# Weights of the last expert layer loaded into free places, two sets during the first expert layer, and their splits moved

## What is computed

```python
def _L2_ffn_ref(x, gate_w, w1, w2, w3, sw1, sw2, sw3):      # first expert layer
    scores = jax.nn.softmax(xf @ gate_w.T, axis=-1)
    topw, topi = jax.lax.top_k(scores, TOP_K)
    h = jax.nn.silu(jnp.einsum('td,eid->tei', xf, w1)) * jnp.einsum('td,eid->tei', xf, w3)
    h = h * comb[:, :, None]
    y = jnp.einsum('tei,edi->td', h, w2)
    z = jax.nn.silu(xf @ sw1.T) * (xf @ sw3.T) @ sw2.T
...
def _L3_attn_ref(x, w_qkv, b_qkv, w_out, b_out):            # attention layer
    attn = jax.nn.softmax(jnp.einsum('bqd,bkd->bqk', q, k) * scale, axis=-1)
    out = jnp.einsum('bqk,bkd->bqd', attn, v)
    return out @ w_out + b_out
...
def _L3_ffn_ref(x, Wr, Wi, bi, Wo, bo):                     # last expert layer
    topk_vals, topk_idx = jax.lax.top_k(router_logits, TOP_K)
    h = jnp.einsum('th,efh->etf', xf, Wi) + bi[:, None, :]
    h = jax.nn.gelu(h, approximate=False)
    expert_out = jnp.einsum('etf,ehf->eth', h, Wo) + bo[:, None, :]
```

## Time and profile before

| | |
|---|---|
| median of 3 runs | 1121.81 us |
| profiled execution, its own time | 1123.41 us |
| its span | 1121.6 us |
| mean granted clock of TensorE | 0.814 of 2.4 GHz |
| PE busy | 869.2 us (77%) |
| DVE busy | 811.3 us (72%) |
| ACT busy | 600.2 us (54%) |
| POOL busy | 341.9 us (30%) |
| DMA moved | 117.88 MB, mean 105 GB/s |
| the attention layer lies at | 896.5 to 976.6 us |
| the last layer begins at | 976.9 us |

### The profile page before, as it was taken

The page is one execution under the profiler, slowest core; times in us unless marked ns, Lnnn a source line. Parts: engine busy times, 40 slices in busy tenths (PEclk is TensorE's granted clock), DMA queues, the critical chain, the costliest instruction groups (busy, mean ns, idle before and its releaser), DMA issues. The chain is left out here.

```text
span 1121.6 us, 17427 instructions
## 1 busy us (share of the span) xinstructions
PE 869.2 (77%) x6016; PEld 586.7 (52%) x6016; DVE 811.3 (72%) x1730; ACT 600.2 (54%) x1009; POOL 341.9 (30%) x337
## 2 busy tenths in 40 slices
PE   7689999986999665577663287999999386557992
PEld 3333333342589512233361265998888344457991
DVE  6589999984754489999937864888886445473763
ACT  2755454412477377799934144677773054265660
POOL 0026666633066122222100023222222600034335
PEclk9889999997999655555556578999999776769995
DMA  8086665503000000000000181999990274302653
GB/s 268 23 229 157 174 173 155 141 1 85 1 1 3 19 0 1 0 1 1 1 1 1 43 238 62 255 267 258 267 265 24 57 194 132 101 26 65 227 203 88
DMA packets 61735, 117.88 MB, mean 105 GB/s; under 512 B 10256, under 2 KB 37456, under 8 KB 61648
## 3 DMA queue, kind: packets, MB, share of 16 engines
q1 hardware_dynamic: 58576, 110.48, 35.1%
q0 software_dynamic: 3072, 6.30, 1.8%
HBM read 91.09 MB, written 16.81 MB: 96 GB/s over the span
## 5 line engine op out<-in xcount | busy, mean ns | idle before, releaser
L459 POOL TENSOR_TENSOR hC<-hs,Cb 128x1024 f32<-128x1024 f32 x47 | 110.9, 2359 | 124.0 <-DVE hs L498 124.0
L498 DVE TENSOR_TENSOR_SCAN hs<-ps_l,dBu 128x1024 f32<-128x1024 f32 x48 | 110.0, 2291 | 2.8 <-ACT ps_l L590 1.2
L658 PE MATMUL ps_l<-hC,selT 128*96 128x512 f32 x192 | 93.3, 609 | 1.5 <-POOL hC L459 1.5
L590 ACT ACTIVATE ps_l<-d_sp,Am 128x1020 f32<-128x1020 f32 x48 | 53.5, 1115 | 71.5 <-DVE hs L498 71.3
L643 PE MATMUL ps_l<-du,sel 96*128 96x512 f32 x192 | 90.5, 593 | 1.4 <-DVE dBu L491 1.4
L1900 POOL CAST m_h_hi<-m_h 128x512 f16<-128x512 f32 x54 | 49.1, 910 | 139.3 <-DVE m_h L1975 139.3
L2304 PE MATMUL ps_m<-m_wd_hi,m_h_hi 128*128 128x192 f16 x248 | 62.3, 251 | 7.3 <-issue 4.0
L1986 DVE TENSOR_TENSOR m_h_lo<-m_h,m_h_hi 128x512 f16<-128x512 f32 x62 | 42.8, 691 | 34.0 <-POOL m_h_hi L1900 31.0
L2191 ACT ACTIVATE m_act<-ps_m 128x512 f32<-128x512 f32 x62 | 36.8, 593 | 56.8 <-PE ps_m L2286 50.9
L1585 PE MATMUL ps_l<-q_xi,identh 128*128 128x512 f16 x48 | 28.5, 595 | 48.9 <-DVE q_ex L1340 28.1
L1213 POOL TENSOR_SCALAR q_e<-q_qi 128x512 int16<-128x512 f16 x48 | 30.0, 625 | 119.1 <-ACT q_qi L1480 60.6
(11 more groups left out here) (543 smaller groups left out, 2862.5 us busy)
## 6 DMA issues: line engine op xcount, KB each, us to landing
d_sp<-scan_d SPq DMA_DIRECT2D x48, 512.0 KB, 4.5
m_sta<-in_m_ua SPq DMA_DIRECT2D x25, 512.0 KB, 4.3
m_stb<-in_m_ub SPq DMA_DIRECT2D x50, 256.0 KB, 5.7
m_std<-in_m_dn SPq DMA_DIRECT2D x25, 384.0 KB, 6.0
gw_dn_in<-gw_dn SPq DMA_DIRECT2D x10, 576.0 KB, 3.3
gw_dn_in<-in_g_dn SPq DMA_DIRECT2D x8, 576.0 KB, 5.5
scratch_x<-zero SPq DMA_DIRECT2D x1, 4416.0 KB, 19.6
m_xg<-scratch_x SPq DMA_DIRECT2D x23, 192.0 KB, 5.9
```

Source lines behind the costliest of these rows:

```text
L459: pool.tensor_tensor(hC[:, n % 2, :], hs[:, n % 2, :], Cb[:, which(n), :], ALU.mult).then_inc(weighted, 1)
L498: v.tensor_tensor_scan(hs[:, n % 2, ::step], dA(n)[:, ::step], dBu[:, n % 2, ::step], 0.0, ALU.mult, ALU.add).then_inc(scanned, 1)
L590: act.activation(dst[:, :, o:o + L - 1], d_sp[:, n % NSP, :].rearrange("p (b t) -> p b t", t=L)[:, :, o:o + L - 1], ACT.Exp, scale=Am[:, c ...
L658: mm = pe.matmul(ps[0:DI, 6 + half, :], selT[:, n % NG, :], hC[:, n % 2, half * BANK:(half + 1) * BANK], start=(n == STEPS), stop=(m == ST ...
```

## The change

The two staging places are allocated before the first expert layer, and sets 0 and 1 are loaded into them by SP during that layer, right after its last own weight set. Sets 2, 3 and 4 are loaded at the start of the attention layer, as raw float32 into the final places of experts 7, 6 and 5 (`raw`, `places`); sets 5, 6 and 7 use the staging places again. Splitting set 5, 6 or 7 overwrites the raw data of set 4, 3 or 2, so its high parts wait for the low parts of those. All 24 splits are now made in the attention layer: high 0 to 2 before the norm's square root, 3 to 5 after the row turns, 6 to 13 one after each evacuation, 14 to 17 before the image loop, 18 to 23 one in each n; low 0 to 13 before the a_v adds, 14 and 15 after them, 16 to 19 one for each image behind its copy, 20 and 21 at n = 5, 22 and 23 at n = 6 behind the last residual add. In the last layer the splits go, `G_DIRECT` becomes 6, and each direct block has a one-hot place of its own, made three blocks ahead.

```diff
-def expert_layer(nc, K, X, D, ln, pre, use, routed, tiles, gated, out=None):
+def expert_layer(nc, K, X, D, ln, pre, use, routed, tiles, gated, R, out=None):
...
                     while ahead < sets and begins[ahead - NST] <= b - 1:
                         load(ahead)
                         ahead += 1
+                        if ahead == sets:
+                            for n in range(2):
+                                R.load(sync, D, n)
...
-G_DIRECT = 5
+G_DIRECT = 6
-G_LATE = 18
...
+    def places(self, ctx):
         self.up = ctx.sb("gw_up", [P, GE, 4, GU], F16)
         self.dn = ctx.sb("gw_dn", [P, GE, 2, GD], F16)
         self.bias = ctx.sb("gw_bias", [P, GE, GT])
+
+    def raw(self, w):
+        if w in (2, 3, 4):
+            up = self.up[:, 9 - w, :, :].rearrange("p a c -> p (a c)").bitcast(F32)
+            dn = self.dn[:, 9 - w, :, :].rearrange("p a c -> p (a c)").bitcast(F32)
+        else:
+            up = self.up_in[w in (1, 6)][:, :, :].rearrange("p a c -> p (a c)")
+            dn = self.dn_in[w in (1, 6)][:, :]
+        return up[:, 0:GU], up[:, GU:2 * GU], dn
 
     def load(self, sync, D, w):
-        a = w % 2
-        if w >= 2:
-            sync.wait_ge(self.lo_done, 3 * (w - 1))
+        if w >= 5:
+            sync.wait_ge(self.lo_done, {5: 3, 6: 6, 7: 18}[w])
...
     def high(self, act, n):
+        w, i = divmod(n, 3)
         src, hi, lo = self.parts(n)
-        act.wait_ge(self.w_in[n // 3 % 2], 64 * (n // 6 + 1))
+        act.wait_ge(self.w_in[w], 64)
+        if w >= 5:
+            act.wait_ge(self.lo_done, 3 * (9 - w) + 3)
         act.activation(hi, src, ACT.Copy, scale=WS).then_inc(self.hi_done, 1)
...
                 def one_hot(b):
-                    if b >= 2:
-                        v.wait_ge(turned, b - 1)
...
-                    if G_LATE + b < 3 * GE:
-                        R.low(v, G_LATE + b)
                     low(2 * b)
-                    if 2 <= b + 2 < G_DIRECT:
-                        one_hot(b + 2)
+                    if b + 3 < G_DIRECT:
+                        one_hot(b + 3)
...
-                for n in range(G_LATE, 3 * GE):
-                    R.high(act, n)
...
             def _(sync):                                   # attention layer
-                for w in range(2):
+                for w in range(2, 5):
                     R.load(sync, D, w)
                 sync.dma_start(R.bias[:, :, :], D["g_b"].rearrange("(e p) f -> p e f", p=P)).then_inc(R.bias_in, 16)
                 clear_last(sync, K)
-                for w in range(2, GE):
+                for w in range(5, GE):
                     R.load(sync, D, w)
...
-                for n in range(8):
+                for n in range(14):
                     R.low(v, n)
                 for q in range(NT // 2):
                     v.wait_ge(vals, q + 1)
                     v.tensor_tensor(vt[:, 2 * q:2 * q + 2, :], ...
-                    if q in (1, 3):
-                        R.low(v, 8 + q // 2)
+                for n in range(14, 16):
+                    R.low(v, n)
...
                         v.tensor_copy(PT[:, b % 2, :, :], ...
+                        R.low(v, 15 + n)
...
-                    for i in range(10 + 2 * n, min(12 + 2 * n, G_LATE)):
-                        R.low(v, i)
+                    if n >= 5:
+                        for i in range(2 * n + 10, 2 * n + 12):
+                            R.low(v, i)
...
             def _(act):
+                for n in range(3):
+                    R.high(act, n)
                 ln.scalar(act, use)
                 tr.scalar(act, use - 2, uT, ps)
+                for n in range(3, 6):
+                    R.high(act, n)
...
-                        if n >= 1:
-                            R.high(act, n - 1)
-                for n in range(7, 10):
+                        R.high(act, 6 + n)
+                for n in range(14, 18):
                     R.high(act, n)
```

More of the change, by code:

```diff
@@ L2360 @@
 G_BLOCKS = GE + G_OVER
-G_DIRECT = 5
+G_DIRECT = 6
 G_TRIO = 3 * P
-G_LATE = 18
 class LastWeights:
     def __init__(self, ctx):
+        self.up_in = [ctx.sb(f"gw_up_in{a}", [P, 2, GU]) for a in range(2)]
+        self.dn_in = [ctx.sb(f"gw_dn_in{a}", [P, GD]) for a in range(2)]
+        self.w_in = [ctx.sem(f"gw_in{w}") for w in range(GE)]
+        self.bias_in = ctx.sem("gw_bias_in")
+        self.hi_done, self.lo_done = ctx.sem("gw_hi"), ctx.sem("gw_lo")
+    def places(self, ctx):
         self.up = ctx.sb("gw_up", [P, GE, 4, GU], F16)
@@ L2379, in load @@
     def load(self, sync, D, w):
-        a = w % 2
-        if w >= 2:
-            sync.wait_ge(self.lo_done, 3 * (w - 1))
-        sync.dma_start(self.up_in[a][:, 0, :], D["g_ua"][w * CA:(w + 1) * CA, :]).then_inc(self.w_in[a], 16)
+        if w >= 5:
+            sync.wait_ge(self.lo_done, {5: 3, 6: 6, 7: 18}[w])
+        a, b, d = self.raw(w)
+        sync.dma_start(a, D["g_ua"][w * CA:(w + 1) * CA, :]).then_inc(self.w_in[w], 16)
         for half in range(2):
-            sync.dma_start(self.up_in[a][half * CB:(half + 1) * CB, 1, :], D["g_ub"][w * CB:(w + 1) * CB, :]).then_inc(self.w_in[a], 16)
@@ L2386, in load @@
-        sync.dma_start(self.dn_in[a][:, :], D["g_dn"][w * P:(w + 1) * P, :]).then_inc(self.w_in[a], 16)
+            sync.dma_start(b[half * CB:(half + 1) * CB, :], D["g_ub"][w * CB:(w + 1) * CB, :]).then_inc(self.w_in[w], 16)
+        sync.dma_start(d, D["g_dn"][w * P:(w + 1) * P, :]).then_inc(self.w_in[w], 16)
     def parts(self, n):
         w, i = divmod(n, 3)
-        if i < 2:
-            return self.up_in[w % 2][:, i, :], self.up[:, w, 2 * i, :], self.up[:, w, 2 * i + 1, :]
-        return self.dn_in[w % 2][:, :], self.dn[:, w, 0, :], self.dn[:, w, 1, :]
+        hi, lo = (self.dn[:, w, k, :] if i == 2 else self.up[:, w, 2 * i + k, :] for k in range(2))
@@ L2394, in high @@
+        return self.raw(w)[i], hi, lo
     def high(self, act, n):
+        w, i = divmod(n, 3)
         src, hi, lo = self.parts(n)
-        act.wait_ge(self.w_in[n // 3 % 2], 64 * (n // 6 + 1))
+        act.wait_ge(self.w_in[w], 64)
+        if w >= 5:
+            act.wait_ge(self.lo_done, 3 * (9 - w) + 3)
         act.activation(hi, src, ACT.Copy, scale=WS).then_inc(self.hi_done, 1)
@@ L2424, in last_layer @@
         seat = ctx.sb("g_seat", [P, NT, GE])
-        hot = ctx.sb("g_hot", [P, 2, NT, P], F16)
+        hot = ctx.sb("g_hot", [P, G_DIRECT, NT, P], F16)
         lg = ctx.sb("g_lg", [P, NT, GE])
@@ L2576, in one_hot @@
                 def one_hot(b):
-                    if b >= 2:
-                        v.wait_ge(turned, b - 1)
                     for t in range(NT):
-                        v.tensor_scalar(hot[:, b % 2, t, :], slots1[:, :], seat[:, t, b:b + 1], None, ALU.is_equal).then_inc(hot_ready, 1)
+                        v.tensor_scalar(hot[:, b, t, :], slots1[:, :], seat[:, t, b:b + 1], None, ALU.is_equal).then_inc(hot_ready, 1)
                 def copy_up(d):
@@ L2643, in _ @@
                 one_hot(1)
+                one_hot(2)
                 v.wait_ge(placed, 2)
@@ L2770, in turn @@
                                 mm = pe.matmul(ps[:, 4 + b % 2, part * P:(part + 1) * P], U16[:, t, part * P:(part + 1) * P],
-                                               hot[:, b % 2, t, :], start=(t == 0), stop=(t == NT - 1))
+                                               hot[:, b, t, :], start=(t == 0), stop=(t == NT - 1))
                     else:
@@ L2965, in _ @@
                                            accum_out=sums[:, 2 * b + q:2 * b + q + 1]).then_inc(expd, 1)
+                        R.high(act, 18 + n)
+                    else:
+                        R.high(act, 18 + n)
                     if n >= 2:
@@ L2972, in _ @@
                                        ACT.Copy).then_inc(out_sb, 1)
-                    for i in range(10 + 2 * n, min(12 + 2 * n, G_LATE)):
-                        R.high(act, i)
             @block.tensor
@@ L3064, in program @@
             quantised_layer(nc, K, X, D, ln)
+        R = LastWeights(ctx)
         if LAYERS > 3:
-            expert_layer(nc, K, X, D, ln, "m", 1, 16, 4, True)
-        R = LastWeights(ctx)
+            expert_layer(nc, K, X, D, ln, "m", 1, 16, 4, True, R)
+        R.places(ctx)
         if LAYERS > 4:
```

## The result

The changed kernel takes 1132.26 us (median, 1130.72 to 1133.03) against 1121.76 (1121.34 to 1123.26) of the kernel before: ratio 1.0092, 95% interval 1.0069 to 1.0115: slower, by just under one per cent. The forecast was 1129.1. Its profiled execution has a span of 1130.8 us, 9.2 more than the 1121.6 of before. One execution among all runs of this document, one of ten of after_dve_dummies (experiment 5), took 3362.59 us, and its ratio leaves that one out.

| us | before | after | difference | predicted |
|---|---|---|---|---|
| first expert layer ends | 896.46 | 908.22 | +11.8 | +11.1 |
| attention layer | 80.44 | 69.52 | -10.9 | -5.0 |
| last layer | 144.7 | 153.06 | +8.4 | +1.2 |
| sum | | | +9.2 | +7.3 |

The account below looks back on a forecast made before the run. It took PE as the bound once DMA ran empty in the first expert layer, a PE, DVE, ACT ring in attention, PE late in the last layer. +11.1 - 5.0 + 1.2 = +7.3 on 1121.81 gave 1129.1 us, range 1117 to 1133.

Parts of the forecast that it names:

- Part 1: First expert layer: two sets loaded ahead of the last m_xg make PE stand 8.9 us, then restart slowly; +11.1 us.
- the restart at the lower clock: First expert layer, behind PE's stall: PE restarts at half clock, costing 1.9 to 3.3 us, taken as 2.2.
- early loads hide: Rival, first expert layer: m_xg is served beside the 2.75 MB, so PE never waits; 1118.0 us, chance 0.14.
- Part 2: Attention layer: loading sets 2, 3, 4 and moving splits gives -9.0 in the rounds, +3.5 at the tail; taken as -5.0.
- the DVE splits (4.2): Attention layer, third and fourth rounds: splits no longer hold DVE ahead of what PE waited for; -4.2 us.
- The tail: Attention layer's end: DVE's splits 20 to 23 around the last add put +3.5 us in front of the block's end.
- The warning signs named: Signs of a wrong forecast, among them set 7 or set 4 arriving late and holding ACT before exp or OT.
- Part 3: Last layer: removed splits count 0, block 5 built by 24 matmuls instead of 3 transposes costs +1.2 us.
- the six low splits of DVE in the loop lie in PE's shadow: 0: Last layer's loop: removing DVE's six low splits changes the time by 0, at most -1 us.
- nothing gained: Last layer: the wait on all scatters moves one block later, but block 5 was turned after it; 0.
- a rival of +4: Last layer: block 5's direct turn lengthens a stretch with unexplained idle time, +4 instead of +1.2; 1132 us, chance 0.08.
- the likeliest case: Whole kernel: the forecast itself, 1129.1 us, own range 1125 to 1132.5, chance 0.72.

Follow-up runs that it names:

- after_dve_dummies: Changed kernel plus six useless DVE instructions of a low split's size in the last layer's blocks 0 to 5: 1128.33 us, ratio 1.0054.
- experiment 5: Third-chip runs: loads_behind_rows, after_direct5 and all_gaps repeated, plus after_dve_dummies; ratios 0.9967, 1.0069, 0.9968 and 1.0054.
- experiment 1: Two, one or no early weight sets put ahead of the first expert layer's last rows: ratios 1.0106 (kernel before otherwise), 0.9877 and 0.9819 (changed kernel otherwise).
- before_again: The kernel before, unchanged, profiled again on the second chip: 1122.11 us (one execution).
- before_early_loads: Kernel before with only weight sets 0 and 1 loaded early, in the first expert layer instead of the attention layer: 1131.73 us, ratio 1.0106.
- second set: Runs on the second chip, among them before_again, after_again and all_gaps, beside the kernel before at a median of 1122.96 us.
- first set: Runs on the first chip, among them before_early_loads, loads_behind_rows and after_direct5, beside the kernel before at a median of 1120.42 us.
- after_direct5: Changed kernel with G_DIRECT back at 5 instead of 6: 1118.31 us, ratio 0.998; repeated on the third chip 1129.8 us, ratio 1.0069.
- loads_behind_rows: Changed kernel with both early weight sets issued behind the last routed block's rows and that step's store: 1100.61 us, ratio 0.9819.
- third set: Runs on the third chip, those of experiment 5, beside the kernel before at a median of 1122.59 us.
- all_gaps: Changed kernel with early sets behind the last rows, first high splits behind the square root, tail low splits in DVE's idle time: 1113.68 us, ratio 0.9922.
- after_again: The changed kernel, unchanged, run again on the second chip: 1132.73 us, ratio 1.0085 against the kernel before.
- loads_behind_second: The kernel of loads_behind_rows repeated on the third chip: 1117.6 us, ratio 0.9967 against the kernel before.

## Why the prediction was right, and where it was not

**Part 1, right.** Each step of it shows in rows. m_xg went out at 838.57 (named: near 839), landed at 852.5 (computed 851.4), PE idled 9.68 (8.9), the layer ended 11.8 later (11.1). What is left of 11.8 behind the stall is 2.1, which I put down to the restart at the lower clock (2.2). The rival "early loads hide" needed a landing before 845. The rule of the Trainium skill ("DMA: Bandwidth & Descriptors", section "Queues, rings and completion order") that each DMA engine consumes descriptors in ring order agrees with the dose of experiment 1: 8.8 to 9.7, 4.0 and no stall for two, one and no sets ahead. The advice in the same page of the Trainium skill, section "Rules for kernel authors", to issue early and wait late, holds here only for loads that have nothing urgent behind them on their queue. Where the loads went behind the rows, it held: ratio 0.982 and 0.997 in two sets.

**Part 2, right in its steps up to the first round, too small behind it.** Counted from the layer's start, to which 11.76 are added: the projections came 0.96 later (+0.9), the scores stood at 928.16 (927.9), exp at 933.31 (933.1), the first transposes 5.25 earlier (4.8). Then the sum was mis-sized. Fourth round's transposes: 11.4 us earlier, not 9.0. The step charged only the DVE splits (4.2) and kept PE's durations. But PE had the higher clock more of the time: windows over the image loop show 0.89 granted where before had 0.74. The shorter gaps (1.51 and 1.37 instead of 3.59 and 3.51) go with it, but they aren't shown to be all of it: before_again, with the same gaps of 3.59 and 3.51, had 0.82. In order after, before, before_again:

```profile
952.00:972.00 20.00, 16.09 (x77) 13.09 (x78) 9.18 (x19) 7.97 (x16) 0.00 (x0) 0.89 0.22 70
```

```profile
945.00:975.00 30.00, 21.39 (x80) 17.18 (x80) 11.14 (x21) 7.98 (x16) 0.00 (x0) 0.74 0.34 97
```

```profile
944.00:972.00 28.00, 19.39 (x81) 15.21 (x80) 11.14 (x21) 7.99 (x16) 0.00 (x0) 0.82 0.38 114
```

So the output products of a round took 1.89 us, and the output projection 1.47, instead of 3.62 and 2.29 in the fourth round of before, and PE's last product of the layer ended 14.4 us earlier, where the forecast had 9.0. The tail was as computed: from that product to the layer's end 4.3 us instead of 0.9, +3.4 (3.5), with DVE's splits 20 to 23 around the last add:

```profile
972.64 1.35 DVE L2420 SCALAR_TENSOR_TENSOR gw_dn<-gw_dn_in,gw_dn 128x1152 f16<-128x1152 f32 x1
973.91 0.95 DVE L2420 SCALAR_TENSOR_TENSOR gw_up<-gw_up_in,gw_up 128x768 f16<-128x768 f32 x1
974.78 0.55 DVE L2950 TENSOR_TENSOR X<-X,ps_l 128x384 f32<-128x384 f32 x1
975.24 0.95 DVE L2420 SCALAR_TENSOR_TENSOR gw_up<-gw_up_in,gw_up 128x768 f16<-128x768 f32 x1
976.11 1.35 DVE L2420 SCALAR_TENSOR_TENSOR gw_dn<-gw_dn_in,gw_dn 128x1152 f16<-128x1152 f32 x1
```

Together (-14.36 and +3.44) that is the -10.9. How much of it belongs to the change is less sure, since the base moves. The profile on which the sum was made had an attention layer of 80.4 us; before_again had 75.6 and before_early_loads, with an unchanged queue order in this layer's DVE and ACT, 75.4. Its projections ran 16.29 us, in the other two 13.97. Within one set the change gave -6.9 (second set, 75.6 to 68.7) and, without the sixth block, -5.8 (first set, 75.4 to 69.6). In both sets the clock of the projections worked against the change: 15.77 against 13.97 in the second, 16.38 against 13.97 in the first. So this part is worth between 6 and 11 us, and the forecast of -5.0 was too small in each pair. The warning signs named (a set landing late) came true in small: ACT waited 0.66 us for set 4 and 1.76 for set 7; what these waits cost wasn't measured.

**Part 3, wrong in size.** The step that failed is "the six low splits of DVE in the loop lie in PE's shadow: 0". Their leaving changed what ran beside them. Where the waits occur, the last layer got longer by 8.4 and 8.1 (146.4 to 154.5 in the second set), and ACT's waits doubled from 8.5 to 16.6. Where they don't occur (first set), it got shorter: 144.0 in before_early_loads, 139.7 in after_direct5, 138.3 and 136.6 in two versions with six direct blocks. There the scatters themselves bind: before the first block whose rows come from DRAM, PE idles 4.44 us in before_early_loads (sixteen scatters, first to last start 22.5 us), 2.93 in after_direct5 (20.0 us), and with six direct blocks not at all. So "0" for the splits and "nothing gained" for the wait on all scatters were both wrong on that chip:

```profile
1031.69 0.33 PE L2780 MATMUL ps_g<-identh,g_xg 128*128 128x128 f16 x3 [4.44 <-DMA g_xg<-scratch_x]
```

```profile
1022.31 0.33 PE L2788 MATMUL ps_g<-identh,g_xg 128*128 128x128 f16 x3 [2.93 <-DMA g_xg<-scratch_x]
```

The sum of ACT's waits isn't a price by itself. The kernel before has 8.2 to 8.5 us of them and a last layer of 144.7 and 146.4, against 144.0 without any (in before_early_loads); loads_behind_rows goes from 138.3 without them to 154.5 with 16.6. The rows of the prediction had the sign of this, with 2.36 us of "issue", and a rival of +4 was built on it; the size lay outside. Experiment 5 shows that DVE work of the splits' size at their place takes back about half. Why ACT and PE don't go on while the scatters run, and why only on some chips or in some sessions, stays open: no row names it. One rival is that the engines' instructions come late; no run tests it. The DMA view has a packet of instructions in the microsecond behind the start of ACT's wait and another behind PE's restart (1005 and 1015 in after), but the first stands at the same place (986) in loads_behind_rows, without a wait. The sixth direct block's own price (+1.2 predicted) changes sign with it: five blocks gave 151.5 in the third set against 154.5 and 155.0 for six, but 139.7 in the first set against 138.3 and 136.6 for six (in kernels that differ in the place of the early loads as well).

**The sum.** +0.7 in part 1, -5.9 in part 2 and +7.2 in part 3 against their forecasts gave +1.9 together. The time lay in the likeliest case's range (1125 to 1132.5) because two errors cancelled, and that is luck; only part 1 was right in mechanism and size. On the first set's chip the change would have been about even, an estimate: with five direct blocks it stood at 0.998 there and at 1.0069 in the third set; the changed kernel itself wasn't run on the first chip.

**A better version.** loads_behind_rows was faster than the kernel before in both its sets, 0.982 and 0.997. all_gaps was in its two, 0.992 and 0.997. In the third set the two stand at 1117.6 and 1118.25, no difference: what all_gaps gives in the attention layer (63.4 and 65.2) over the other (67.4 and 65.0) wasn't there twice. The clock hides part of it: in the third set the projections of all_gaps ran 16.04 us, those of the other 13.97.

## What to carry to other kernels

A load that is issued early is free for the consumers of its data and not for what stands behind it on the queue: look for the next small read that an engine wants, put the bulk behind it, and price the other order by bytes over measured rate. Work that hides in another engine's shadow may still pace a neighbour, so check what runs beside it before its removal is booked at zero. Make the sum per stage and compare the stages afterwards, with a second profile of the kernel before; a right total can hide two wrong terms.

## What the runs showed of the hardware

- While 16 scatters run on POOL, ACT can stand still for most of 16.6 us and PE with it, and PE has gaps of 0.4 to 1.2 us inside a row of 24 products, with all named inputs there. In six profiles of kernels without DVE splits in this stretch (after, after_again, all_gaps and three of the third set) the sum was 16.57 to 16.66; in all four profiles of the first set it was nothing, and without scatters (one profile) nothing.
- With DVE instructions of 0.95 to 1.35 us beside the scatters, single ones take up to 2.3 us instead of 0.97, and ACT's waits are 9.0 us instead of 16.6.
- 192 KB behind 2.75 MB on one queue land 11.6 to 13.9 us after the issue (seven profiles), behind 1.38 MB 9.5, and 7.1 to 8.9 with neither set ahead (six profiles).
- After 9.7 us without work PE ran at granted clock 0.50 from 852.5 up to 856 and 1.00 from 858 on; with the waits of the last layer the clock is low again (0.50, 0.69 and 0.73 in the three stretches of 4 us from 992 to 1004 in loads_behind_second).
- One unchanged kernel's attention layer measured 80.4 and 75.6 us in two profiles, with granted clocks of 0.65 and 0.99 in the first 8 us of its projections.
